# First batch of a decoder layer reordered, and its combiner product made in three passes

## What is computed

```python
x = x + attn(layernorm(x), queries, combiners)        # products of x with itself, no softmax
x = x + xattn(layernorm(x), ctx, ctx, Wq, bq, Wk, bk, Wv, bv)   # softmax((qWq+bq)(kWk+bk)^T/sqrt(512)) (vWv+bv)
x = x + ffn(layernorm(x), router, experts, shared)    # top 2 of 16 experts, with capacity
```

## Time and profile before

| | us |
|---|---|
| median of 3 runs | 1844.45 (1843.58 to 1847.43) |
| profiled execution | 1844.15 |
| its span | 1842.4 |
| PE busy | 1823.9 |
| DVE, ACT, POOL busy | 831.8, 751.1, 895.0 |
| DMA over the span | 115 GB/s |

### The profile page before, as it was taken

One profiled execution on the slowest core, in us unless ns is written; L12 is line 12 of the kernel. 1 busy time (PEld: TensorE's weight loads), 2 busy tenths in 40 slices (PEclk: granted clock), 3 DMA queues, 4 the chain that ended last, 5 costly groups with the idle time before them and its releaser, 6 DMA issues.

```text
span 1842.4 us, 26986 instructions
## 1 busy us (share of the span) xinstructions
PE 1823.9 (99%) x10048; PEld 1606.4 (87%) x10048; DVE 831.8 (45%) x2013; ACT 751.1 (41%) x1486; POOL 895.0 (49%) x764
## 2 busy tenths in 40 slices
PE   8999999999999999999999999999999999999997
PEld 5888888888887787888899999999999999999996
DVE  5567556755764344443344234432444324443242
ACT  4444444434463333332444344443444434444331
POOL 5343444244544233224656666565655656556631
PEclk9999999999999999999999999999999999999999
DMA  8221323133352223332766667666576675666622
GB/s 320 95 91 57 115 101 101 46 115 109 102 139 36 47 46 81 47 46 54 173 124 163 150 141 145 131 163 152 136 144 138 160 155 132 138 143 164 146 39 29
DMA packets 215218, 212.56 MB, mean 115 GB/s; under 512 B 133520, under 2 KB 133520, under 8 KB 214704
## 3 DMA queue, kind: packets, MB, share of 16 engines
q1 hardware_dynamic: 189792, 157.73, 31.6%
q0 software_dynamic: 25296, 53.11, 16.7%
HBM read 132.51 MB, written 48.92 MB: 98 GB/s over the span
## 4 chain that ended last, share of the span: by engine, by line
PE 98%; DVE 1%; ACT 0%; issue 0%; DMA 0%; POOL 0%; SPq 0%; ACTq 0%; DVEq 0%; POOLq 0%
PE ps L71 65%; PE ps L1453 23%; PE ps L815 4%; PE ps L902 2%; PE ps L821 1%; PE ps L939 1%; PE ps L838 1%; DVE buffer L652 0%; ACT buffer L453 0%; DMA buffer<-in_WkT 0%; PE ps L883 0%; DVE buffer L680 0%; DVE stats L592 0%; ACT buffer L448 0%; DVE buffer L693 0%
## 5 line engine op out<-in xcount | busy, mean ns | idle before, releaser
L71 PE MATMUL ps<-buffer,buffer 128*128 128x320 f32 (+1 forms) x6816 | 1225.6, 340 | 1.2 <-DVE buffer L680 0.9
L71 PEld LDWEIGHTS ps<-buffer,buffer 128*128 128x128 f32 x6816 | 1104.7, 188 | 106.6 <-issue 4.9
L1209 POOL TENSOR_TENSOR buffer<-buffer,buffer 128x512 fp32r<-128x512 f32 x289 | 379.7, 1480 | 249.5 <-ACT buffer L1267 249.1
L1453 PE MATMUL ps<-buffer,buffer 128*128 128x512 f32 x1904 | 437.6, 390 | 0.2 <-DVE buffer L1355 0.2
L1453 PEld LDWEIGHTS ps<-buffer,buffer 128*128 128x128 f32 x1904 | 355.8, 188 | 74.5 <-issue 1.1
L1267 ACT ACTIVATE buffer<-buffer 128x512 fp32r<-128x512 f32 (+1 forms) x491 | 293.8, 651 | 164.3 <-PE ps L1453 93.8
L1309 ACT ACTIVATE buffer<-ps 128x320 f32<-128x320 f32 (+1 forms) x240 | 112.5, 469 | 599.8 <-PE ps L71 566.7
L1371 DVE TENSOR_TENSOR ps<-ps,buffer 128x320 f32<-128x320 f32 (+2 forms) x198 | 100.2, 506 | 488.7 <-ACT buffer L1309 475.5
L1256 POOL DMA_INDIRECT out_tokens<-buffer,slot_list x80 | 125.8, 1573 | 185.5 <-DVE buffer L1401 177.7
L440 POOL DMA_INDIRECT slots<-pairs,slot_u x64 | 63.6, 994 | 182.0 <-DVE slot_u L802 164.9
L448 ACT ACTIVATE buffer<-ps 128x512 fp32r<-128x512 f32 (+1 forms) x148 | 81.6, 601 | 116.1 <-PE ps L71 39.8
(11 more groups left out here) (116 smaller groups left out, 1094.8 us busy)
## 6 DMA issues: line engine op xcount, KB each, us to landing
buffer<-in_wts SPq DMA_DIRECT2D x289, 256.0 KB
buffer<-in_x SPq DMA_DIRECT2D x8, 1024.0 KB, 6.5
buffer<-in_xT SPq DMA_DIRECT2D x8, 1024.0 KB, 5.1
buffer<-in_ctxT SPq DMA_DIRECT2D x8, 1024.0 KB, 8.0
out_tokens<-buffer SPq DMA_DIRECT2D x8, 1024.0 KB, 4.3
tokens_normed<-buffer SPq DMA_DIRECT2D x32, 256.0 KB, 2.8
out_tokens<-buffer POOLq DMA_DIRECT2D x32, 256.0 KB, 6.2
buffer<-means SPq DMA_DIRECT2D x8, 256.0 KB, 4.3
```

Of the source, the lines that this page charges most:

```text
L71: last = pe.matmul(out, left, right, start=(c == 0 and i == 0), stop=(c == len(parts) - 1 and i == 2))
L1209: pool.tensor_tensor(wl[n % RING][:], wraw[n % RAW][:], wh[n % RING][:].bitcast(F32), ALU.subtract).then_inc(s_wl, 1)
L1453: ins = pe.matmul(down_bank[n % 2][:], left, right, start=(c == 0 and i == 0), stop=(c == FC - 1 and i == len(passes) - 1))
```

## The change

In the first batch:

- POOL makes the tile of ones first, and PE runs 28 matmuls of 128 x 128 on it (`WARM`) ahead of everything.
- x of batch 0 is loaded in four tiles between the weight loads, each with a semaphore. CT is loaded behind the store of the means instead of ahead of it. x of batch 2 is loaded later (`QBIAS`).
- W moves to banks 2 to 5 and A(0) to 6, 7, 0, 1. The last four matmuls of W, one for each column block, are `INIT`, `INIT1`, `INIT2`, `INIT3` and stand behind the first three row blocks, behind G, behind T and behind M. V(0) waits for the last one's low part.
- LN0 stands ahead of WV. The centring of batch 0 is on DVE (`centre`).
- `KEY` is only the four key sums, multiplied and summed in one instruction each on DVE. The products with bq remain POOL's and their sums ACT's, in a step of their own, `QBIAS`, behind Y1T(0). `fill_tables` is the step `FILL`.
- `XB` (POOL's addition of bv) of batch 0 moves behind the statistics of batch 1.

From the second batch on, T is made in three passes: in `SPLIT` and `LOW` ACT and DVE split CT in ct_hi and ct_lo, G is split in g_hi (ACT) and g_lo (DVE). The place of ct_hi is overwritten by the probabilities, so it is stored once in DRAM and loaded again behind every A from batch 1 on.

```diff
+WARM = 28
-            "W": (5, 6, 7, 0), "LP": (6,), "LX": (7,), "X": (7,)}
+            "W": (2, 3, 4, 5), "LP": (6,), "LX": (7,), "X": (7,)}
+    COLUMN = {"INIT": 0, "INIT1": 1, "INIT2": 2, "INIT3": 3}
+    OTHER_BANK = {("Q", B - 1): (6, 7, 0, 1), ("A", 0): (6, 7, 0, 1)}
...
-            if j == 1:
-                load_x(0)
+            for t in range(2 * j, min(2 * j + 2, NT)):
+                sp.dma_start(x[0][:, t, :], a["x"][0, t * P:(t + 1) * P, :]).then_inc(s_x0[t], 16)
...
             if name == "KEY":
-                sp.wait_ge(s_summed, NC)
+                sp.wait_ge(s_key_sums, 1)
...
+                if b >= 1:
+                    sp.dma_start(ct_hi[:].bitcast(F32), combiners).then_inc(s_ct_loaded, 16)
...
         def step(name, b):                                  # gpsimd
             if name == "MEAN":
-                pool.wait_ge(s_xT, 16 * (b + 1))
+                if b >= 1:
+                    centre(pool, b)
+            if name == "FILL":
+                fill_tables()
+            if name == "QBIAS":
+                pool.wait_ge(s_wk_rows, 32)
+                pool.wait_ge(s_stat[1], 1)
                 for c in range(NC):
+                    pool.tensor_tensor(wk_rows[:, c, :], wk_rows[:, c, :], bq_row[:], ALU.mult).then_inc(s_biased, 1)
...
-            if name == "KEY":                               # scalar
+            if name == "QBIAS":
+                for c in range(NC):
+                    row_sum(qbias[:, c:c + 1], wk_rows[:, c, :], c + 1)
+                row_sum(qbias[:, NC:NC + 1], bq_row[:], NC + 1)
...
+            if name == "KEY":                               # vector
+                dve.wait_ge(s_wq_rows, 32)
+                for c in range(NC):
+                    last = dve.tensor_tensor_reduce(krow_products[:, c, :], wq_rows[:, c, :], bk_row[:], 1.0, 0.0,
+                                                    ALU.mult, ALU.add, key_sums[:, c:c + 1])
+                last.then_inc(s_key_sums, 1)
...
+            if name == "G" and b >= 1:                      # vector
+                dve.wait_ge(s_g_hi, b)
+                dve.tensor_tensor(g_lo[:], bank[:], g_hi[:].bitcast(F32), ALU.subtract).then_inc(s_ev["G"], 1)
...
+        for _ in range(WARM):                               # tensor
+            pe.matmul(ps[BANKS - 1][:, 0:P], ones[:], ones[:], start=True, stop=True)
...
             if name == "V":
                 if b == 0:
+                    drained(pe, "W", 0, NC - 1)
...
+                    else:                                   # T, b >= 1
+                        ins = three_pass(pe, bank_of("T", b, q)[:],
+                                         [(g_hi[:, cols], g_lo[:, cols], ct_hi[:, q, :], ct_lo[:, q, :])])
...
+            steps = [("ST0", 0), ("LN0", 0), ("WV", 0), ("INIT", 0), ("MEAN", 0), ("G", 0), ("INIT1", 0), ("T", 0),
+                     ("C", 0), ("INIT2", 0), ("M", 0), ("KEY", 0), ("INIT3", 0), ("FILL", 0), ("A", 0), ("LN1", 0)]
```

More of the change, by code:

```diff
@@ L237, in phase1 @@
     s_wqk, s_wv = [sem(f"s_wqk{j}") for j in range(NC)], sem("s_wv")
-    s_x = [sem(f"s_x{i}") for i in range(XS)]
+    s_x0, s_x = [sem(f"s_x0_{t}") for t in range(NT)], [sem(f"s_x{i}") for i in range(XS)]
     s_c = sem("s_c")
@@ L498, in step @@
                     copy(VWH[:, c, :], wv_raw[:, c, :]).then_inc(s_wh, 1)
-            if name == "INIT":
-                for c in range(NC):
-                    filled(act, "W", 0, c)
-                    bank = bank_of("W", b, c)
-                    copy(WH[:, c, :], bank[:]).then_inc(s_whi, 1)
+            if name in COLUMN:
+                c = COLUMN[name]
+                filled(act, "W", 0, c)
+                bank = bank_of("W", b, c)
+                copy(WH[:, c, :], bank[:]).then_inc(s_whi, 1)
             if name == "Y1T":
                 if b == 0:
-                    act.wait_ge(s_summed, 2 * NC + 1)
+                    act.wait_ge(s_key_sums, 1)
                 for c in range(NC):
@@ L536, in step @@
                        .then_inc(s_qh, 1)
+            if name == "SPLIT":
+                for q in range(H):
+                    copy(ct_hi[:, q, :], CT[:, q, :]).then_inc(s_ct_hi, 1)
             if name == "G":
@@ L833, in step, with product @@
         def step(name, b):
-            if name == "INIT":
-                for j in range(NC):
-                    pe.wait_ge(s_wqk[j], 32)
-                    for c in range(NC):
-                        last = pe.matmul(bank_of("W", b, c)[:], wq_raw[:, j, c * P:(c + 1) * P], wk_raw[:, j, :],
-                                         start=(j == 0), stop=(j == NC - 1))
-                        if j == NC - 1:
-                            last.then_inc(s_mm["W"], 1)
+            if name in COLUMN:
+                def product(j, c):
+                    return pe.matmul(bank_of("W", b, c)[:], wq_raw[:, j, c * P:(c + 1) * P], wk_raw[:, j, :],
+                                     start=(j == 0), stop=(j == NC - 1))
+                if name == "INIT":
+                    for j in range(NC - 1):
+                        pe.wait_ge(s_wqk[j], 32)
+                        for c in range(NC):
+                            product(j, c)
+                    pe.wait_ge(s_wqk[NC - 1], 32)
+                product(NC - 1, COLUMN[name]).then_inc(s_mm["W"], 1)
             if name == "V":
```

113 lines of the change are left out of this document (69 added, 44 removed).

## The result

| us | before | after |
|---|---|---|
| median, 5 runs each | 1843.86 (1843.58 to 1847.43) | 1852.87 (1850.90 to 1853.63) |
| profiled execution | 1844.15 | 1850.9 |
| its span | 1842.4 | 1849.2 |

The ratio of the changed kernel to the one before is 1.0045, interval 1.0034 to 1.0057: slower by 0.3 to 0.6%. I had forecast 1844.4, with a range up to 1849.0. The profiled execution of the changed kernel is the fastest of its five, and that of the kernel before lies 0.3 us above its median, so the spans differ by 6.8 us where the medians differ by 9.0; the traces account for the 6.8. A stand is a stretch in which an engine does nothing.

A forecast was written before the change was run, and what follows sets the result against it. PE's own work and its stands were taken to bound the kernel (98% of the chain). Terms of +3.1, +1.7 and -4.8 us summed to 0.0, so 1844.4 us; own range 1840.5 to 1847.5, with rivals 1837.5 to 1849.0.

The forecast's parts named there:

- Term one: Before V(0): early fills delay bk, so V(0) starts 3.1 us later, with ends at -3.5 and +3.9.
- my 42.1: Forecast start of V(0) in us: KEY starting at 36.6 plus 5.5 of DVE work; 39.0 before.
- The store of means waits in the same queue ...: no starvation: First batch's loads: CT, xT and QT still fill the queue while the store waits, so no cost was added.
- Centring on DVE at 0.62 each: Batch 0 before V(0): four at 0.62 us with POOL still, ending well before bk lands; upper bound 1.67 each.
- From KEY on the steps: DVE before V(0): four key sums 2.7, low part 0.6, three A additions 2.0, release 0.2; together 5.5 us.
- Term two: From V(0) to G(1): late five sums delay batch 1's normalisation, so G(1) starts later, +1.7 us (0 to 2.7).
- LOW at 2.5 us: Between V(0) and G(1): the combiner's four low parts on DVE take 2.5 us, ending before Q's copies.
- a sign of being wrong: The forecast is wrong if V(0) starts before 38 us or a new stand appears in batches 1 to 7.
- Term three: T in seven batches: three passes instead of 8 loads save 0.68 us each, -4.8 us in all.
- rival 3: T: three passes give nothing because the second half of G's copy is late; 1849.2 us, chance 0.05.
- Rival 1: Before V(0): fills don't hold up the loads; V(0) at 35.5, 1837.8 us; half effect 1841.1, chance 0.30.
- Rival 2: Before V(0): starved loads make PE stand and its clock halve, slowing A and V; +4 us, 1848.5, chance 0.17.

The follow-up runs named there:

- e4: The changed kernel with only the slot table's fill (80 KB) moved behind the key sums, the two large fills still early; 1848.48 us.
- e1: The changed kernel with all three fills issued only after the key sums; 1841.76 us, ratio to before 0.9973 to 0.9992.
- e10: The changed kernel with only the slot table filled early and the two large fills behind the key sums; 1845.44 us.
- e9: The kernel before with only the three-pass combiner (its split, store and reload) added; 1838.99 us, ratio to before 0.9956 to 0.9981.
- e3: The changed kernel with XB of batch 0 moved behind the centring of batch 1; 1852.42 us.
- e5: The changed kernel with fills behind the key sums, XB behind batch 1's centring, and DVE's wait for ACT's five sums moved later; 1838.93 us.
- e8: The e5 kernel with 36 matmuls on ones ahead of A(0) and 36 ahead of V(0); 1837.80 us.
- e7: The e5 kernel without the 28 matmuls on ones; 1837.52 us.

## Why the prediction was wrong

**Term one failed** (+3.1 us forecast, +8.7 measured), and its mechanism was half right. I had seen that the fills move ahead of the loads, and had priced their 2.70 MB by bytes at 6.4 us; the large two cost 6.6 (e4 against e1). Three steps beside it failed:

- The fills were counted by their bytes alone. The slot table was 3% of them and cost 4.6 us by e4 (3.6 by e10), as the rate of everything beside it halved. This is most of the 5.6 us between my 42.1 and the 47.7.
- "The store of means waits in the same queue ...: no starvation" looked at whether the engines have work, not at who waits for the store. It lands behind all that was issued ahead of it (the weights and Wv; CT, xT and QT, which I had named, come behind it), and that got a third of the bytes, and SP issues the reload, the context, Wq and bk only when it has landed. So bk landed at 40.5 where I had 36.4, and DVE, which stood until the means had landed at 34.8, was not ready for it before 42.5: the delay reached V(0) by the means and the centring, where I had it come by bk.
- Centring on DVE at 0.62 each: it took 1.04, or 4.1 us for four, with POOL idle beside it. In the changed kernel it ended at 38.9, 1.5 us behind the landing of the context and not "well before bk lands"; I estimate that it cost up to 1.5 us there.

The 1.1 us by which e1's V(0) (36.6) lies above my 35.5 for undelayed loads are not the centring's, as DVE waited for the context after it. There bk landed at 30.9 where I had 30.0, and KEY began 0.5 us behind it, after the context's low parts.

From KEY on the steps held: from its start to V(0) 5.24 us, against 5.5.

**Term two** (+1.7, measured +1.46) was right in place and size: DVE waited for the five sums until V(0) + 17.0 (forecast 17.1), G(1) started at V(0) + 25.7 (forecast 26.0), released by L478. **But the same paragraph had LOW at 2.5 us** and didn't cost the move of XB: +1.76 us, a stand ahead of the score tile, which I had named as a sign of being wrong. The rows to see it by were there: L652 beside POOL takes 1.67 each. I had used them for KEY's neighbours and not for LOW's.

**Term three** (-4.8, measured -5.1) was right, and e9 shows it by itself, which also answers rival 3. The store and the reloads show no cost beside it. Of the sum, then, two terms held, one was 5.6 us too low, and a stand that it didn't have added 1.8.

**Rivals.** Rival 1 (V(0) at 35.5 if the fills don't hold up the loads) is what e1 makes true: 36.6. It gave 1841.8 and not 1837.8, since V took 1.6 us longer at the lower clock behind two stands, XB cost 1.8, and V(0) came 1.1 later. Rival 2 had the direction right and the wrong lever. PE did stand before V(0) as it said, 2.37, 3.56, 1.27 and 3.29 us, and the clock fell:

```profile
14.00:16.00 2.00, 1.75 (x4) 0.83 (x5) 0.00 (x0) 2.00 (x3) 0.00 (x0) 0.86 1.04 420
16.00:18.00 2.00, 2.00 (x4) 0.85 (x3) 0.00 (x0) 0.86 (x2) 0.00 (x0) 0.50 1.03 414
```

T was slowed as well (5.40 us instead of 3.67). But both low stretches were over before the means had landed at 34.8, which gated V(0) anyway, and A and V ran at the upper level (3.84 and 11.16 us). In e1 and e10 the same effect did reach the path, with V at 12.8 us. The early matmuls and the weight products in the gaps bring nothing while DVE gates V(0), as forecast.

## What to carry to other kernels

When an edit moves a DMA, list every transfer that stands in the queues while it runs and ask for each which engine waits for its landing: a 2 KB store behind a megabyte may release the loads that everything needs. Price a transfer by its packets as well as by bytes, and distrust one in very small pieces. And price a moved vector instruction beside what GpSimd does in its new place, with the row for that, not with the row of its old place.

## What the runs showed of the hardware

- Where both queues had work they got nearly the same number of packets, 68 and 69 in one microsecond and much the same in each from 9 to 18 us (after), so 4 KB packets took twice the bytes of 2 KB ones (0.28 and 0.14 MB). In the half microsecond of the kernel before it was 31 and 47. The Trainium skill ("DMA: Bandwidth & Descriptors", Queues, rings and completion order) has the engines change between queues by packet; the trace of the changed kernel agrees, and the consequence is in the sizes.
- Beside 80 KB in pieces of 40 bytes all that the engines moved fell from 404 to 248 GB/s over 6 us (e10 against e1, 8 to 14 us), and from 349 to 440 down to 181 to 235 over 6 us when they ran behind the large fills (after against e4, 18 to 24 us).
- A store of 2 KB landed 0.5 to 0.7 us behind the megabyte issued ahead of it on the same queue, whether that took it 4.8 us (e1) or 14.0 (after).
- DVE beside POOL's multiplications and additions: a key sum 1.77 us instead of 0.68, a low part 1.4 (after, beside XB) instead of 0.62 (e3).
- The granted clock went to its 1.2 GHz level after stands of about 2 us (2.37 in after, 1.83 and 1.88 in e1, 2.15 in e5) and of 3.11 us (e10), and the fall was seen between at once (e5) and 1.4 us (e1) after PE had taken up work again. In e8, with matmuls in the stands, it did not fall. Stands of 3.29 us (after) and 2.26 us (e7) ahead of V(0) were followed by no fall (V 11.16 and 11.13 us), so the length of the stand alone doesn't decide.
